# Second expert layer: scattering expert rows as accumulating DMAs into a sums buffer, instead of storing them and adding them on VectorE

## The reference

```python
x = x + 0.5 * ffn(layernorm(x), router_weight, gate_up_proj, gate_up_bias, down_proj, down_bias)
x = x + attention(layernorm(x), Wq, bq, Wk, bk, Wv, bv, Wo, bo)
x = x + 0.5 * ffn(layernorm(x), router_weight, gate_up_proj, gate_up_bias, down_proj, down_bias)
```

## Time and profile before

| | before |
|---|---|
| median of 3 runs | 704.48 us |
| span of the profiled execution | 799.3 us |
| first gather of the second layer | 517.3 us |
| first and last scatter of the second layer start | 542.3 and 761.4 us |
| first load of `y_dram` after it | 763.6 us |
| end of the span | 799.3 us |
| TensorE busy / VectorE / ScalarE / GpSimd | 79% / 56% / 39% / 44% of the span |

### The profile page before, as it was taken

How to read it: one execution, slowest core, us unless ns; L and a number is a source line. 1 busy time by engine, 2 the same in 40 slices (tenths; PEclk the granted TensorE clock), 3 DMA queues, 4 the chain that set the end, 5 groups by cost and what they waited for, 6 DMA issues and landing times.

```text
span 799.3 us, 13210 instructions
## 1 busy us (share of the span) xinstructions
PE 631.0 (79%) x3712; PEld 527.1 (66%) x3713; DVE 446.0 (56%) x1116; ACT 314.2 (39%) x696; POOL 353.5 (44%) x379
## 2 busy tenths in 40 slices
PE   2673898888878879969998996679898898888900
PEld 2452777776757668858887994568777786767700
DVE  6868653444434436277775986845353444445446
ACT  2663243434333335346663443334243334333400
POOL 2781646565656553513331000155656565656400
PEclk9985999999999998999999999599988999999955
DMA  9871232222222221245542431132212222222179
GB/s 307 295 229 28 73 99 81 70 78 69 85 72 78 78 73 52 93 135 157 157 142 94 150 116 66 8 87 67 79 62 85 70 82 69 79 72 79 54 261 369
DMA packets 52601, 87.99 MB, mean 110 GB/s; under 512 B 16228, under 2 KB 32019, under 8 KB 52054
## 3 DMA queue, kind: packets, MB, share of 16 engines
q1 hardware_dynamic: 17568, 39.52, 15.0%
q0 software_dynamic: 13664, 35.42, 14.3%
q10 hardware_dynamic: 21334, 12.61, 5.1%
HBM read 53.94 MB, written 35.39 MB: 112 GB/s over the span
## 4 chain that ended last, share of the span: by engine, by line
PE 61%; DVE 13%; another core or an unknown queue 8%; DMA 7%; issue 5%; ACT 4%; POOL 0%; SPq 0%; ACTq 0%; DVEq 0%; POOLq 0%
PE ps L854 15%; PE ps L852 13%; PE ps L853 12%; PE ps L843 9%; PE ps L1070 3%; DMA work<-y_dram 3%; PE ps L847 3%; DVE aT_lo L1447 2%; PE ps L877 2%; ACT aT_hi L689 2%; DVE xs L1503 1%; DMA raw_c<-L_ffn_down_proj 1%; PE ps L926 1%; PE ps L869 1%
## 5 line engine op out<-in xcount | busy, mean ns | idle before, releaser
L521 POOL DMA_INDIRECT y_dram<-work,sidx x142 | 142.7, 1005 | 166.7 <-ACT work L706 128.7
L513 POOL DMA_INDIRECT work<-xn_dram,gidx x142 | 140.2, 988 | 47.2 <-issue 43.6
L1455 DVE TENSOR_SCALAR work<-ps 128x256 f32<-128x256 f32 x142 | 57.1, 418 | 147.3 <-issue 83.3
L843 PE MATMUL ps<-cst,work 128*128 128x128 f32 x688 | 109.4, 284 | 29.9 <-DVE aT_lo L1447 22.5
L852 PE MATMUL ps<-up_hi,xT_hi 128*128 x284 | 120.9, 426 | 13.5 <-issue 11.2
L854 PE MATMUL ps<-up_hi,xT_lo 128*128 x284 | 114.1, 402 | 8.6 <-issue 8.2
L853 PE MATMUL ps<-up_lo,xT_hi 128*128 x284 | 113.8, 401 | 8.5 <-issue 7.8
L696 ACT ACTIVATE work<-ps 128x256 f32<-128x256 f32 x142 | 52.1, 393 | 171.7 <-PE ps L854 129.8
L843 PEld LDWEIGHTS ps<-cst,work 128*128 128x128 f32 x688 | 84.3, 145 | 52.3 <-issue 35.3
L852 PE MATMUL ps<-dn_hi,aT_hi 128*128 x284 | 96.7, 340 | 0.0
L706 ACT ACTIVATE work<-ps,slot_gate 128x256 f32<-128x256 f32 x142 | 59.5, 471 | 72.2 <-PE ps L854 54.7
(11 more groups left out here) (172 smaller groups left out, 1136.5 us busy)
## 6 DMA issues: line engine op xcount, KB each, us to landing
work<-y_dram SPq DMA_DIRECT2D x32, 512.0 KB, 4.3
xn_dram<-work ACTq DMA_DIRECT2D x29, 255.0 KB, 2.6
xs<-L_attn_x SPq DMA_DIRECT2D x4, 1024.0 KB, 10.5
work<-q_dram SPq DMA_DIRECT2D x16, 256.0 KB, 2.8
out<-xs SPq DMA_DIRECT2D x16, 256.0 KB, 5.9
q_dram<-work ACTq DMA_DIRECT2D x15, 256.0 KB, 2.3
work<-xn_dram,gidx POOLq DMA_INDIRECT x142
y_dram<-work,sidx POOLq DMA_INDIRECT x142
```

The source lines that it names most:

```text
L513: pool.indirect_dma_start(xg[:, k, u, 1:H + 1], None, xn_dram[n], bass.IndirectOffsetOnAxis(ap=gidx[:, 2 * s + u:2 * s + u + 1], axis=0)). ...
L521: pool.indirect_dma_start(y_dram[n], bass.IndirectOffsetOnAxis(ap=sidx[:, 2 * s + u:2 * s + u + 1], axis=0), ysb[:, k, u, :], None, bounds ...
L843: ins = nc.tensor.transpose(ps[:, bank, k:k + P], src[:, u, c * P:(c + 1) * P], ident)
L1455: return v.tensor_scalar(upv[:, u, :], ps[:, 2 + 2 * b + u, :].rearrange("p (f c) -> p f c", c=2)[:, :, 1], 1.0 - LIMIT, 1.0 + LIMIT, ALU. ...
```

## The change

In the second layer alone:

- a DRAM buffer `sums_dram` of 4096 + 128 rows takes the place of the layer's `y_dram`;
- in the second pass SyncE's queue stores each pair of `xs`, once the attention's output has been added, to `sums_dram` (16 DMAs of 256 KB);
- `sidx` is now the token's row itself, and an empty slot goes to one of 128 spare rows, its own for each partition; three VectorE instructions in `route` compute it;
- each scatter adds its rows to those of `sums_dram` (an accumulating indirect DMA without a bounds check), and waits until the scatter before it has landed, since two tiles of different experts can hold the same token; the very first waits for the 16 stores;
- GpSimd's queue takes gather and scatter in turn (u = 0, then u = 1) instead of two gathers and two scatters;
- at the end four DMAs of 1 MB copy `sums_dram` to the output, DRAM to DRAM; the 16 loads of `y_dram`, the 32 VectorE additions and the 16 stores of `xs` are gone.

The first layer keeps its order and its operations.

```diff
-        y_dram = [scratch(f"y_dram{n}", [T * TOPK, H]) for n in range(2)]
+        y_dram = scratch("y_dram", [T * TOPK, H])
+        sums_dram = scratch("sums_dram", [T + P, H])
...
+        def part(rows, q):
+
+            n = T // OUT_PARTS
+            return rows[q * n:(q + 1) * n, :].rearrange("(p i) h -> p (i h)", p=P)
...
+            with sp.Fori(0, NG) as g:
+                sp.wait_ge(x_done, g + 1)
+                sp.dma_start(pair(sums_v, g), pair(xs, g)).then_inc(sums_begun, 16)
+
             wait_scattered(1)
-            for j in range(4):
-                sp.dma_start(ybuf[:, j], pair(y_v[1], j)).then_inc(L[1].y_loaded[j], 16)
-
-            def finish(g, j, more):
-                sp.wait_ge(L[1].y_used, g + 1)
-                if more:
-                    sp.dma_start(ybuf[:, j], pair(y_v[1], g + 4)).then_inc(L[1].y_loaded[j], 16)
-                sp.dma_start(pair(out_v, g), pair(xs, g)).then_inc(out_stored, 16)
...
+            for q in range(OUT_PARTS):
+                sp.dma_start(part(out_rows, q), part(sums_dram, q)).then_inc(out_stored, 16)
+            sp.wait_ge(out_stored, 16 * OUT_PARTS)
...
+                def scatter(s, u):
+                    k = s % RING
+                    rows = bass.IndirectOffsetOnAxis(ap=sidx[:, 2 * s + u:2 * s + u + 1], axis=0)
+                    pool.wait_ge(l.y_sb, evicted(s, u))
+                    if n == 0:
+                        pool.indirect_dma_start(y_dram, rows, ysb[:, k, u, :], None, bounds_check=T * TOPK - 1,
+                                                oob_is_err=False).then_inc(l.scattered[k], 16)
+                        return
+                    if s == 0 and u == 0:
+                        pool.wait_ge(sums_begun, 16 * NG)
+                    elif u == 0:
+                        pool.wait_ge(l.scattered[(s - 1) % RING], 32 * ((s - 1) // RING + 1))
+                    else:
+                        pool.wait_ge(l.scattered[k], 32 * (s // RING) + 16)
+                    pool.indirect_dma_start(sums_dram, rows, ysb[:, k, u, :], None, compute_op=ALU.add
+                                            ).then_inc(l.scattered[k], 16)
...
+                    for u in range(2):
+                        if s + RING < NP and u < halves(s + RING):
+                            gather(s + RING, u)
+                        if s >= 2:
+                            scatter(s - 2, u)
...
+                if n == 1:
+                    spare = small[:, 6:7]
+                    st.done(v.tensor_scalar(spare, cst[:, C_P:C_P + 1], 0.5, float(T), ALU.mult, ALU.add))
+                    st.done(v.tensor_scalar(nam[:, 0, :], nam[:, 1, :], 0.0, spare, ALU.is_equal, ALU.mult))
+                    st.done(v.tensor_tensor(sidx[:, :], gidx[:, :], nam[:, 0, :], ALU.add))
...
-            def last_body(it):
-                for j in range(4):
-                    combine(l1, it * 4 + j, j, it)
-            st.loop(NG // 4, 4, last_body)
```

More of the change, by code:

```diff
@@ L327, in __init__ @@
                 self.y_ps, self.y_sb = s("y_ps"), s("y_sb")
-                self.y_loaded = [s(f"y_loaded_{j}") for j in range(4 if n else 2)]
+                self.y_loaded = [s(f"y_loaded_{j}") for j in range(0 if n else 2)]
                 self.y_used = s("y_used")
@@ L517, in scatter @@
-                def scatter(s):
-                    k = s % RING
-                    for u in range(halves(s)):
-                        pool.wait_ge(l.y_sb, evicted(s, u))
-                        pool.indirect_dma_start(y_dram[n],
-                                                bass.IndirectOffsetOnAxis(ap=sidx[:, 2 * s + u:2 * s + u + 1], axis=0),
-                                                ysb[:, k, u, :], None, bounds_check=T * TOPK - 1,
-                                                oob_is_err=False).then_inc(l.scattered[k], 16)
@@ L526, in experts @@
-                for s in range(RING):
-                    gather(s)
+                    pool.indirect_dma_start(xg[:, k, u, 1:H + 1], None, xn_dram[n],
+                                            bass.IndirectOffsetOnAxis(ap=gidx[:, 2 * s + u:2 * s + u + 1], axis=0)
+                                            ).then_inc(first_tile_in if s == 0 and u == 0 else l.gathered[k], 16)
+                def scatter(s, u):
[14 more added lines that the diff above has]
+                                            ).then_inc(l.scattered[k], 16)
@@ L528, in experts @@
+                for s in range(RING):
+                    for u in range(halves(s)):
+                        gather(s, u)
                 for s in range(NP):
@@ L530, in experts @@
                         pool.wait_ge(l.x_lo, turned(s))
-                        gather(s + RING)
-                    if s >= 2:
-                        scatter(s - 2)
+                    if n == 0:
+                        if s + RING < NP:
+                            for u in range(halves(s + RING)):
+                                gather(s + RING, u)
+                        if s >= 2:
+                            for u in range(2):
+                                scatter(s - 2, u)
+                        continue
+                    for u in range(2):
+                        if s + RING < NP and u < halves(s + RING):
+                            gather(s + RING, u)
+                        if s >= 2:
+                            scatter(s - 2, u)
                 for s in range(NP - 2, NP):
-                    scatter(s)
+                    for u in range(halves(s)):
+                        scatter(s, u)
             experts(0)
```

23 lines of the change are left out of this document (8 added, 15 removed).

## The result

The changed kernel takes 838.66 us (median of 4 runs, 835.3 to 838.81) against 704.14 for the kernel before (4 runs, 702.71 to 705.45). The ratio is 1.190, interval 1.187 to 1.193: 134.5 us slower, where 729 and a range of 687 to 785 were forecast. The direction was right, the size was not.

A forecast was written before the change was run, and what follows sets the result against it. The prediction took TensorE, with GpSimd close behind, to bound the second layer's expert stage and DMA the tail. The scatter chain's +43 us and the tail's -18.9 took 704.5 to 729 us, range 687 to 785.

The forecast's parts named there:

- The mechanism: Second layer's scatters: each waits for the landing before it, at an even pitch of about 3.2 us, TensorE gaps about 1.2.
- The stage without the chain: Second layer's expert stage, first to last scatter start without stalls: 183 us, with TensorE at 5.28 us a step.
- The plain landing: Second layer's scatter without the add: lands 2.10 us after its start.
- The add: Accumulating scatter over a plain one: 0.50 us for a DRAM read plus 0.37 for 131 KB more, landing 2.97.
- Release to start: From one scatter's landing to the next one's start: 0.26 us as for a gather, 0.84 as upper end.
- rival D: Scatter chain: the add is a second transfer or GpSimd's part grows; pitch 4.31 or 4.46 us, 804 or 815; chance 0.18.
- The tail: After the last scatter's start: DMA-bound loads, additions and stores give way to copies, 37.9 us to 19.0, so -18.9 us.
- The copies: Four DRAM to DRAM copies of 4.19 MB at the end: 16 us, between 14.2 and 27.7.
- The order, the stores: Gather and scatter in turn on GpSimd: nothing; 16 stores to the sums buffer in the second pass: nothing, at most +3 us.
- the three VectorE instructions: Instructions added in routing: 0.75 us, hidden in VectorE's 4.90 us of idle time, so nothing.
- Rival A: Scatter chain hidden behind GpSimd's order and TensorE: pitch under the 2.88 us break-even, 689 to 694 us; chance 0.28.
- The prediction's last sentence: If the profiled stalls also happen in normal runs, the chain costs about 7 us and the time is near 693.

The follow-up runs named there:

- e1: Changed kernel with the add taken out of its scatters, every landing wait kept: 736.46 us, ratio 1.046 to the kernel before.
- e4: Kernel before, with gather and scatter taken in turn on GpSimd in the second layer: 706.23 us against 704.1, ratio 1.002.
- e8: Changed kernel whose scatters add only the first 128 features of each row: 858.62 us where the kernel before takes 801.69.
- e10: Kernel before with the second layer's expert rows written, scattered and read back as bf16: 698.91 us, ratio 0.991 to the kernel before.
- A: The changed kernel itself, all parts of the change together: 838.66 us, ratio 1.190 to the kernel before.
- e12: Changed kernel with the two waits ahead of each scatter exchanged, run beside the changed kernel: 799.33 us against its 840.37, kernel before 704.64.
- e3: Changed kernel with plain scatters to rows of their own and no waits between them: 683.64 us, ratio 0.972 to the kernel before.
- e5: Kernel before with only the 16 early stores of xs to a sums buffer added: 800.38 us against 801.69, ratio 0.997.
- e14: Changed kernel without the add and with its two waits exchanged, second run: 788.96 us against 798.76 for the kernel before, ratio 0.985.
- e13: Kernel before with bf16 expert rows in the second layer and eight load buffers instead of four: ratio 0.994 where the kernel before takes 798.76.
- e17: Kernel before with bf16 expert rows in the second layer and four load buffers, run again: ratio 0.992 where the kernel before takes 808.48.
- e6: Changed kernel with the two waits ahead of each scatter exchanged, first run: 858.82 us where the kernel before takes 801.69, ratio 1.069.
- e2: Changed kernel with accumulating scatters to rows of their own that do not wait for one another: 718.01 us, ratio 1.021 to the kernel before.

## Why the prediction was wrong

**The cost of a link was mis-sized in both of its terms, landing and release to start; that is nearly the whole error.** The forecast had a landing of 2.97 and 0.26 to the next start, 3.23 us; the profile after has 3.8 and 0.8, 4.68 from start to start. 70 x (4.68 - 3.23) = 101.5 us of the 109.7 between 729 and 838.7; the stage's own pace, forecast as 183 and measured as 177, is another 6. The mechanism, its place and its consequences were as written: an even pitch, waits ended by the scatter's own landing, TensorE in gaps, a full ring. Term by term:

- *The plain landing*, 2.10 in the forecast: 2.4 in e1. The rows read were those of scatters with skipped slots (e1 and e4).
- *The add*, 0.87 in the forecast as a DRAM read and 131 KB more: 3.8 - 2.4 = 1.4. GpSimd's instruction grew by 0.6 (0.99 to 1.59), which the forecast kept as 0.5 for its upper end only. If that 0.6 goes into the landing in full, the other 0.8 is close to the 0.87 for read and bytes, but no run separates the two, and the split between read and bytes does not look as forecast: half the bytes take 0.49 us off an accumulating link (e8) and 0.17 off a plain landing (2.46 in e4, 2.29 in e10), so the add's own part by the byte is, as an estimate, 2 x 0.32 = 0.64, not 0.37. The DMA queues of the pages of e1 and of A show one more side of it (packets, MB, share of the engines):

```profile
q0 software_dynamic: 13664, 36.34, 16.1%
```
```profile
q0 software_dynamic: 20480, 36.34, 20.7%
```

  The two kernels differ in the add alone and move the same bytes on this queue; with 71 of the scatters accumulating there are 96 more packets for each such scatter, which fits 128 packets of one row each in place of 32 packets of four rows. How much of the landing that costs was not tried.
- *Release to start*, 0.26 in the forecast, for which I took the gather's row over the scatter's 0.84, since the bounds check and its move would go. The move went, but the second wait put a semaphore instruction in its place, and the price from landing to start stayed at 0.80 (e1). What sets it is whether the DMA instruction itself carries the wait that ends last (e12: 0.27, and 41.0 us less), as the gather's does. The upper end that I set aside, 0.84, was the right row for the kernel as written.
- With 0.84 and 0.5 together the forecast's rival D had 4.31 us and 804, chance 0.18. It was the right case and still short: both of its terms came true together, and the plain landing under them was 0.3 longer.

**The stage without the chain**: 183 us forecast; e3 and e4 have 177. **The tail**: -18.9 forecast; in A's profile 38.6 - 19.1 = 19.5 less than in e4's (704.1 - 665.5), in e3, with the faster landing of a plain scatter, 20.5 us in the time. The copies alone were to take 16 and take 15, while the landing before them takes 3.8 for 3.0: that the sum of 19.0 meets 19.1 is in part luck. The Trainium skill's rate for copies between HBM tensors ("DMA: Bandwidth & Descriptors", section "Latency and other measured facts"), 207 to 214 GB/s, was weighed against this; it is for tiles of another layout, and the window after has 278 GB/s, so the measurement decides for the faster figure. **The order, the stores**: nothing, as forecast (e4, e5); **the three VectorE instructions** were not tried by themselves. Put together, 704.1 + (327.3 - 177) - 19.5 = 834.9, 3.8 below the measured time: in A's profile the first scatter starts 1.1 us later than in e4's (489.7 and 488.7), and e4's profiled execution took 706.9 us, 2.8 above the 704.1.

**Rival A's break-even**, 2.88 us a link, lies between what was measured: 3.30 is slower (e1), 2.7 is faster (e14, where before takes about 800). With the measured stage and tail it is (177 + 20.5) / 70 = 2.82.

**A wrong reading that cost little.** The 94.8 us between the profile and the median were put down to the profiler. They are not its doing: the kernel before also takes 799 to 808 us in runs without the profiler (beside e5 to e8 and e13 to e17), and one and the same chip gave medians of 801.69 and 704.64. In the profiles ScalarE's longest waits grow with it. Here are its waits for TensorE's up product in the second expert stage, first where before takes about 800 (e5), then where it takes 704 (e4): us in total, times, the longest:

```profile
ACT work L704 <- PE ps L862: 48.1, 29, 3.9
```
```profile
ACT work L704 <- PE ps L862: 46.2, 65, 1.0
```

So ScalarE is not the one that stalls; it waits for TensorE. The window of e5's stage, beside e4's above, has TensorE busy for 192 us in place of 174 and a granted clock of 0.95 in place of 1.00:

```profile
546.00:762.00 216.00, 192.23 (x1143) 162.91 (x1141) 101.97 (x233) 84.68 (x202) 125.24 (x125) 0.95 0.24 73
```

Taking the stalls out of the stage was still right for a comparison with 704. What causes them is open; nothing here was made to find it. What the change costs where before takes about 800 was not measured for A itself; e6's ratio, 1.069 there against 1.132, shows that part of the stalls disappears behind the chain. The prediction's last sentence, that such stalls in normal runs would bring the change to about 693, is not borne out: e6, with the shorter link of 4.1 us, takes 57 us more than before there.

**How the 155 us above e3 split.** By the waits first: the waits alone 52.8 (e1 - e3), the add on top 102.2. By the add first: the add alone 34.4 (e2 - e3), the waits on top 120.6. Neither part, as A's program has it, is bearable by itself against a tail worth 20.5; together they cost 68 us more than the two alone, since each link pays the longer landing only when something waits for it.

## What to carry to other kernels

An operation that must land before the next may start costs its full landing plus the way to the next start each time; multiply that sum by the number of links and set it against the stage's own pace before looking at bytes or bandwidth. On a queue that is already nearly full, price the instruction as well: 0.6 us more on 71 instructions lost more than the whole tail gave. And where an indirect DMA on GpSimd has two waits, as here, try the one that ends last as the first that the program names: it was worth 41 us.

## What the runs showed of the hardware that was not expected

- An accumulating indirect DMA of 128 rows of 1 KB took 1.59 us on GpSimd against 0.99 plain, and still 1.47 with 64 rows; it landed 3.8 us after its start against 2.4, and 71 of them added 6816 packets to the queue (96 each).
- An indirect DMA behind a semaphore instruction started about 0.76 us after it, 0.80 after the landing waited for (e1), and 0.27 after the landing where it carried that wait itself (e12). The order of two waits in the program decided which.
- A copy of 4.19 MB from DRAM to DRAM in four DMAs of 8 KB a partition took 15 us, 278 GB/s counted once.
- One and the same kernel took 704 us at some times and 799 to 808 at others, on one chip both.
